# An MLP cut into pieces that stand between the attention tiles of two transformer layers

## The reference

```
# layer 0
h = ada_rms(x, cond, ln1_w, ln1_tw)
q, k, v = h @ Wq.T, h @ Wk.T, h @ Wv.T          # 8 query heads of 64, 1 key/value head
q, k = rope(q), rope(k)
x = x + softmax(q k / 8) v @ Wo.T               # within each entry of 64 tokens
h = ada_rms(x, cond, ln2_w, ln2_tw)
x = x + (silu(h @ Wg.T) * (h @ Wu.T)) @ Wd.T    # 512 -> 2048 -> 512
# layer 1
h = layernorm(x) * (1 + scale(cond)) + shift(cond)
q = h @ Wq1.T                                   # 16 query heads of 32
c_kv = h @ Wkd.T                                # latent of 128
k, v = c_kv @ Wku.T, c_kv @ Wvu.T               # 4 key/value heads
out = x + softmax(rope(q) rope(k) / sqrt(32)) v @ Wo1.T
```

## Time and profile before

| | |
|---|---|
| median of 3 timed runs | 1047.96 us (1046.9 to 1049.42) |
| span of the profiled execution | 1046.1 us |
| TensorE matmul busy | 934.1 us, 89% |
| VectorE busy | 575.7 us, 55% |
| ScalarE busy | 356.5 us, 34% |
| GpSimd busy | 219.1 us, 21% |
| mean granted TensorE clock | 0.960 |
| moved by DMA | 30.72 MB |

### The profile page before, as it was taken

One profiled execution on the slowest core, in us unless ns is written; L12 is line 12 of the kernel. 1 busy time (PEld: TensorE's weight loads), 2 busy tenths in 40 slices (PEclk: granted clock), 3 DMA queues, 4 the chain that ended last, 5 costly groups with the idle time before them and its releaser, 6 DMA issues.

```text
span 1046.1 us, 17609 instructions
## 1 busy us (share of the span) xinstructions
PE 934.1 (89%) x6400; PEld 790.3 (76%) x6400; DVE 575.7 (55%) x1019; ACT 356.5 (34%) x749; POOL 219.1 (21%) x174
## 2 busy tenths in 40 slices
PE   3889888988999999999999999999975788888876
PEld 3877777776888888888888888888865777777764
DVE  3056666663444444444444444444455688878884
ACT  4136555553221212112221122211124455555531
POOL 1324444541111101111211112111012122212210
PEclk9679999998999999999999999999997899999998
DMA  8400000000411001010110101100000000000000
GB/s 289 161 1 2 1 0 0 0 1 1 141 31 31 0 30 30 30 30 0 66 40 30 30 0 30 30 0 0 1 1 1 1 23 21 21 10 20 21 22 31
DMA packets 30741, 30.72 MB, mean 29 GB/s; under 512 B 3696, under 2 KB 20976, under 8 KB 30704
## 3 DMA queue, kind: packets, MB, share of 16 engines
q1 hardware_dynamic: 30704, 30.22, 8.9%
HBM read 26.02 MB, written 4.19 MB: 29 GB/s over the span
## 4 chain that ended last, share of the span: by engine, by line
PE 71%; issue 9%; DVE 8%; ACT 5%; POOL 4%; DMA 1%; ACTq 0%; SPq 0%; DVEq 0%; POOLq 0%
PE ps L397 21%; PE ps L399 21%; PE ps L398 21%; PE ps L405 3%; POOL yl L376 2%; DVE ex L803 1%; PE ps L474 1%; DVE xres L814 1%; DVE ex L794 1%; ACT yf L1118 1%; DVE smx L791 1%; DVE smx L798 1%; PE ps L631 1%; PE ps L565 1%; ACT ex L1028 1%
## 5 line engine op out<-in xcount | busy, mean ns | idle before, releaser
L397 PE MATMUL ps<-h2h,mwh 128*128 128x512 f32 x512 | 199.4, 389 | 0.0
L398 PE MATMUL ps<-h2h,mwl 128*128 128x512 f32 x512 | 199.2, 389 | 0.0
L399 PE MATMUL ps<-h2l,mwh 128*128 128x512 f32 x512 | 199.2, 389 | 0.0
L823 DVE TENSOR_TENSOR af<-ps,sg 128x512 f32<-128x512 f32 x64 | 44.3, 692 | 225.4 <-issue 212.4
L832 DVE TENSOR_TENSOR xres<-ps,xres 128x512 f32<-128x512 f32 x256 | 159.1, 682 | 2.1 <-PE ps L399 2.0
L344 POOL TENSOR_TENSOR mwl<-mst,mwh 128x1536 fp32r<-128x1536 f32 x16 | 56.1, 3509 | 373.1 <-ACT mwh L1062 373.1
L1068 ACT ACTIVATE sg<-ps 128x512 f32<-128x512 f32 x64 | 38.2, 598 | 216.8 <-PE ps L399 216.7
L398 PEld LDWEIGHTS ps<-h2h,mwl 128*128 128x128 f32 x512 | 96.1, 188 | 20.0
L399 PEld LDWEIGHTS ps<-h2l,mwh 128*128 128x128 f32 x512 | 96.1, 188 | 19.9
L397 PEld LDWEIGHTS ps<-h2h,mwh 128*128 128x128 f32 x512 | 96.1, 188 | 19.9
L1072 ACT CAST ah<-af 128x512 fp32r<-128x512 f32 x64 | 39.8, 621 | 188.1 <-DVE af L823 188.1
(11 more groups left out here) (161 smaller groups left out, 1737.8 us busy)
## 6 DMA issues: line engine op xcount, KB each, us to landing
mst<-WgT SPq DMA_DIRECT2D x16, 256.0 KB, 2.7
mst<-WuT SPq DMA_DIRECT2D x16, 256.0 KB, 3.1
mst<-WdT SPq DMA_DIRECT2D x16, 256.0 KB, 3.4
out<-fin SPq DMA_DIRECT2D x16, 256.0 KB, 2.0
xres<-x SPq DMA_DIRECT2D x1, 2560.0 KB, 20.9
adaw<-ln_twT SPq DMA_DIRECT2D x2, 1024.0 KB, 9.4
adaw<-adaT SPq DMA_DIRECT2D x1, 2048.0 KB, 14.6
wst<-WqT SPq DMA_DIRECT2D x1, 1024.0 KB, 9.1
```

Of the source, the lines that this page charges most:

```text
L397: pe.matmul(dst, lh, rh, start=start, stop=False)
L398: pe.matmul(dst, ll, rh, start=False, stop=False)
L399: return pe.matmul(dst, lh, rl, start=False, stop=stop)
L823: dve.tensor_tensor(af[:, :], bank(3 + r % 2), sg[:, :], ALU.mult).then_inc(m_af, 1)
```

## The change

The three stages become one. The MLP's outer loop now runs over the four blocks of 512 tokens and the inner one over the 16 groups, so the first block can be worked on when only the first four tiles have left layer 0's attention. Its work is written as a generator `mlp()` on each engine that stops (`yield`) after each piece: gate (12 matmuls), the first half of the step before's down (6), up (12), the other half (6). There are 256 pieces. `fill(pieces, count)` puts the next ones between the parts of the attention tiles, in numbers given by `FILL0` (three places in a step of layer 0) and `FILL1` (five places in a step of layer 1).

- The weights of a group are loaded, rounded and split once per block, 64 times instead of 16, gate and up as one array `gu` that is laid out on the host, down apart. `h2h` and `h2l` hold two blocks instead of four.
- `PREP0`, `LATE_PREP` and `PREP1` say in which step a tile's MLP input is made. The inputs of tiles 12 to 15 are made within layer 1's steps.
- Attention of both layers uses banks 0 to 3 (`XB`), the MLP 4 to 7: one for gate, one for up, two for down. Tiles 13 and 15 of layer 1 use banks 4 to 7 (`YB`).
- The small matmuls of the adaptive scales are spread over steps 0 to 3 (`adaptive_later`).
- Layer 1's latent is folded away: four matmuls of `Wkd` with the key and value weights (`keys_values_weights`) make weights of 256 columns, and `qkv1` has 24 matmuls of 384 columns. `latent_T`, `keys_values`, `key_rope` and the splits of the latent go. The repeated keys are summed by GpSimd (`rope_sum1`).
- Layer 1's output is summed into `xres` and stored from there.
- All hardware loops become straight code.

```diff
-TB_TOKENS = 512
...
+TB = 512
...
+FILL0 = {5: (4, 4, 4), **{s: (4, 4, 4) for s in range(6, 15)}, 15: (4, 5, 4)}
+FILL1 = {-1: (1, 4, 0, 4, 3), **{u: (3, 2, 2, 2, 2) for u in range(0, 9)}, 9: (3, 2, 2, 2, 3)}
+
+PREP0 = {2: 0, 3: 1, 4: 2, 6: 4, 7: 5, 8: 6, 9: 7, 11: 8, 12: 9, 13: 10, 14: 11}
+LATE_PREP = {4: 3}
+PREP1 = {0: 12, 1: 13, 2: 14, 3: 15}
...
+def fill(pieces, count):
+    for _ in range(count):
+        next(pieces, None)
...
+        XB = (0, 1, 2, 3)
+        BG, BU, BD = 4, 5, (6, 7)
+        YB = (4, 5, 6, 7)
...
+            def load_group(n):
+                g, i = n % NG, n % 2
+                wait(sp, m_gul, n - 1)
+                sp.dma_start(rgu[i][:, :], gu[g, :, :]).then_inc(ld_gu[i], 16)
+                wait(sp, m_wdl, n - 1)
+                sp.dma_start(rwd[i][:, :], WdT[g * P:(g + 1) * P, :]).then_inc(ld_wd[i], 16)
...
+            def down(n, i_from, i_to):
+                pe.wait_ge(m_al, n + 1)
+                pe.wait_ge(m_wdl, n + 1)
...
+                for i in range(i_from, i_to):
+                    wait(pe, m_x, n * TPB + i - 1)
+                    f = slice(P * i, P * (i + 1))
+                    three(bank(BD[i % 2]), ah[n % 2][:, f], al[n % 2][:, f], wdh[n % 2][:, :],
+                          wdl[n % 2][:, :], True, True).then_inc(m_down, 1)
+
+            def mlp():
+                for n in range(NN):
...
+                    pe.wait_ge(m_gul, n + 1)
+                    for w, to_bank, done in ((0, BG, m_gate), (1, BU, m_up)):
+                        if w == 0:
+                            wait(pe, m_sg, n)
+                        else:
+                            wait(pe, m_af, n)
+                        for k in range(KT):
+                            f = slice(P * (KT * w + k), P * (KT * w + k + 1))
+                            mm = three(bank(to_bank), guh[i][:, f], gul[i][:, f], h2h[b % 2][:, k, :],
+                                       h2l[b % 2][:, k, :], k == 0, k == KT - 1)
+                        mm.then_inc(done, 1)
+                        yield
+                        if n:
+                            down(n - 1, 2 * w, 2 * w + 2)
+                            yield
...
+            for s in range(-2, NT):
+                f1, f2, f3 = FILL0.get(s, (0, 0, 0))
+                if in_layer(s):
+                    scores(s)
+                if in_layer(s + 1):
+                    qkv(s + 1)
+                if s in PREP0:
+                    pe.wait_ge(a_ds, s + 1)
+                    x2_T(PREP0[s], XB[3])
+                fill(pieces, f1)
+                if in_layer(s):
+                    p_T(s)
+                if in_layer(s - 1):
+                    project(s - 1)
+                adaptive_later(s)
+                fill(pieces, f2)
+                if s == NT - 1:
+                    keys_values_weights()
+                if in_layer(s + 1):
+                    qk_T(s + 1)
+                if in_layer(s):
+                    context(s)
+                if in_layer(s + 2):
+                    x_T(s + 2)
...
+                fill(pieces, f3)
+            for u in range(-1, NT + 1):
+                f1, f2, f3, f4, f5 = FILL1.get(u, (0,) * 5)
+                if in_layer(u):
+                    scores1(u)
+                fill(pieces, f1)
+                if in_layer(u + 1):
+                    qkv1(u + 1)
+                if u == -1:
+                    project(NT - 1)
+                if in_layer(u - 1):
+                    project1(u - 1)
+                fill(pieces, f2)
+                if in_layer(u):
+                    p_T1(u)
+                fill(pieces, f3)
+                if in_layer(u + 1):
+                    qk_T1(u + 1)
+                if in_layer(u):
+                    context1(u)
+                if in_layer(u + 2):
+                    y_T(u + 2)
+                fill(pieces, f4)
...
+                fill(pieces, f5)
...
+            def mlp():
+                for n in range(NN):
+                    yield
+                    if n:
+                        add_down(n - 1, 0)
+                        add_down(n - 1, 1)
+                        yield
+                    dve.wait_ge(m_sg, n + 1)
+                    dve.wait_ge(m_up, n + 1)
+                    wait(dve, m_ah, n)
+                    wait(dve, m_al, n)
+                    dve.tensor_tensor(af[:, :], bank(BU), sg[:, :], ALU.mult).then_inc(m_af, 1)
+                    if n == 0:
+                        low_act(n)
+                    yield
+                    if n:
+                        add_down(n - 1, 2)
+                        low_act(n)
+                        add_down(n - 1, 3)
+                        yield
...
+                if in_layer(u + 2):
+                    stats1(u + 2)
+                if in_layer(u):
+                    softmax_sub1(u)
+                    softmax_norm1(u)
+                if in_layer(u + 2):
+                    mean_rstd(u + 2)
+                fill(pieces, f1)
+                if in_layer(u + 1):
+                    rope_mul1(u + 1)
```

More of the change, by code:

```diff
@@ L297, in _ @@
+            sp.wait_ge(w1f, 1)
+            sp.dma_start(w1st[:, :].rearrange("p (k n) -> p k n", k=KT), by_row(Wo1T)).then_inc(ld_w1, 16)
+            for u in range(0, NT + 1):
+                done += sum(FILL1.get(u, ()))
+                while n < min(done // 4 + 3, NN):
+                    load_group(n)
+                    n += 1
+                if u:
+                    store(u - 1)
+            assert n == NN
+            sp.wait_ge(b_st, 16 * NT)
         @block.gpsimd
@@ L385, in clear_bdv1 @@
+                wait(pool, b_qkT, t)
+                for c in range(2):
+                    key = lambda tile: tile[:, c, 8:10, :].unsqueeze(2).broadcast_to([P, 2, 4, HD1])
+                    pool.tensor_tensor(kr1[:, c, :, :, :], key(u1), key(u2), ALU.add)
+                query = lambda tile: tile[:, :, 0:8, :].rearrange("p c h d -> p c (h d)")
+                pool.tensor_tensor(qr1[:, :, :], query(u1), query(u2), ALU.add).then_inc(b_qks, 1)
             def clear_bdv1():
-                pool.wait_ge(m_x, NG * NT)
+                pool.wait_ge(a_rope, NT)
@@ new lines, in _ @@
+            for u in range(-1, NT):
+                f1, f2, f3, f4, f5 = FILL1.get(u, (0,) * 5)
+                ready, soon = PREP1.get(u), PREP1.get(u + 1)
+                if in_layer(u + 2):
+                    rstd1(u + 2)
+                fill(pieces, f1)
+                if in_layer(u + 1):
+                    rope_sum1(u + 1)
+                fill(pieces, f2 + f3)
+                if in_layer(u + 2):
+                    low_y(u + 2)
+                fill(pieces, f4)
+                if ready is not None:
+                    low_h2(ready)
+                if soon is not None:
+                    rstd2(soon)
+                if u == -1:
+                    low_w1_out()
+                fill(pieces, f5)
@@ L541, in _ @@
-            run_tiles(pe, NT, [(x_T, 2), (scores, 0), (qkv, 1), (x2_T, -2), (p_T, 0),
-                               (project, -1), (qk_T, 1), (context, 0)],
-                      {0: adaptive_rest, NT: lambda: gate_up(0, 0, 0, True),
-                       NT + 1: lambda: gate_up(0, 1, 0, True)})
-            pe.wait_ge(a_gf, NT)
-            down(0, 0, 0)
-            for r in range(2, NBLK):
-                gate_up(0, r, 0, True)
-                down(r - 1, (r - 1) % 2, 0)
-            with pe.Fori(0, NG // 2 - 1) as pair:
-                group(pair * 2 + 1, 1)
-                group(pair * 2 + 2, 0)
@@ L553, in _ @@
-            group(NG - 1, 1)
-            def y_T(t):
-                wait(pe, b_xn, t.n + 1)
-                if isinstance(t.n, int) and t.n == 0:
-                    pe.wait_ge(m_af, NG * NBLK - 1)
-                else:
-                    wait(pe, b_yf, t.n)
-                    wait(pe, b_ch, t.n - 3)
-                    wait(pe, b_cl, t.n - 3)
-                for k in range(KT):
-                    mm = pe.transpose(y_bank(t)[:, P * k:P * (k + 1)], yn[:, P * k:P * (k + 1)], idn[:, :])
-                mm.then_inc(b_xT, 1)
@@ new lines, in _ @@
+            for u in range(-1, NT):
+                f1, f2, f3, f4, f5 = FILL1.get(u, (0,) * 5)
+                ready, soon = PREP1.get(u), PREP1.get(u + 1)
+                if in_layer(u):
+                    softmax_exp1(u)
+                fill(pieces, f1)
+                if in_layer(u + 2):
+                    norm1(u + 2)
+                if in_layer(u + 1):
+                    values1(u + 1)
+                fill(pieces, f2)
+                if in_layer(u):
+                    probs_T1(u)
+                fill(pieces, f3)
+                if in_layer(u + 1):
+                    queries_keys1(u + 1)
+                if in_layer(u):
+                    high_ctx1(u)
+                if in_layer(u + 2):
+                    scale_shift_y(u + 2)
+                    high_y(u + 2)
+                fill(pieces, f4)
+                if ready is not None:
```

(8 more changed lines are left out.)

1301 lines of the change are left out of this document (689 added, 612 removed).

## The result

The changed kernel takes 1055.26 us (median of 4, 1051.89 to 1056.71), the kernel before 1047.43 beside it: a ratio of 1.0070, 95% interval 1.0052 to 1.0088. Run again later, unaltered, it took 1054.76 (ratio 1.0060, 1.0038 to 1.0082). It is 0.7% slower where I forecast 3% faster. The time lies within the range, at its upper end; the sign is wrong.

A forecast was written before the change was run, and what follows sets the result against it. TensorE has nothing to issue for about 155 us, nearly all outside the MLP. Start 132, filled work 751, stalls 26 and tail 105 sum to 1014, plus 1.9: 1016 us, 3% less, range 985 to 1056.

The forecast's parts named there:

- Filled work: TensorE's own time in the filled steps: 109 us in layer 0, 120 in layer 1, 522 for the MLP, 751.
- Stalls: TensorE's waits in the filled steps, mainly down matmuls for VectorE in layer 1 and in step 15: 26 us, bounds 0 and 88.
- Weights per block: Loading, rounding and splitting MLP weights 64 times instead of 16, on DMA, ScalarE and GpSimd: costed at 0.
- Table loads and straight code: 42 Exp/Silu table loads in ScalarE's idle time, 0, bound 54 us; unrolled loops, 0, left to the range.
- Start: Unfilled steps 0 to 4 of layer 0, 13.4 us each, plus small matmuls and half clock: filled steps start at 132 us.
- Tail: Unfilled tiles 10 to 15 of layer 1, steps of 15 to 19 us: 105 us, bounds 90 and 118.
- the first: Rival: TensorE never waits in the filled part and the clock recovers, 983 us; chance 0.20.
- the third: Rival: each of 42 ScalarE table loads delays a softmax or gate by 1.28 us, up to 1070 us; chance 0.05.
- The second: Rival: VectorE's order costs each of 21 filled steps, 4.2 us each giving 1078, 3.5 on average 1064; chance 0.17.
- The fourth: Rival: start at 145 and tail at 118 eat the gain, no change against the kernel before; chance 0.06.
- signs of being wrong: Tile 5's scores below 122 or above 142; waits for weights, DMA or Silu; over 3 us per filled step; tail over 118.
- Layer 1's step 10: Sign of being right: step 10, the first unfilled one in layer 1, begins at about 909 us.

The follow-up runs named there:

- kernel 11: Changed kernel with the edits of experiment 5, weight splits held as in experiment 10, step 15's query-weight split held too: 976.7 us, ratio to kernel before 0.9310.
- experiment 8: Changed kernel with GpSimd's low halves of MLP weights cut to 16 columns for the last 48 of 64 groups: 1041.5 us, ratio to kernel before 0.9935.
- experiment 10: Changed kernel with GpSimd's gate and up weight splits held until VectorE has formed `al` of two groups before: 1044.6 us, ratio to kernel before 0.9972.
- Experiment 1: Changed kernel with VectorE doing the first filling's MLP work before softmax reciprocal and scaling in layer 1: 1025.5 us, ratio to kernel before 0.9802.
- experiment 7: Changed kernel with Silu replaced by Identity, so the 42 table loads of the filled steps go: 1053.1 us, ratio to kernel before 1.0027.
- Experiment 6: Changed kernel with all 96 small matmuls ahead of tile 0's scores again: 1059.2 us, ratio to kernel before 1.0105.
- experiment 3: Changed kernel with own PSUM banks and an earlier input transpose in layer 0's steps 0 to 4: 1034.8 us, ratio to kernel before 0.9885.
- experiment 4: Changed kernel with tiles 11, 13, 15 on the other banks and earlier transposes for tiles 12 to 15: 1035.6 us, ratio to kernel before 0.9907.
- experiment 5: Changed kernel with the edits of Experiment 1, experiment 3, experiment 4, and GpSimd's statistics first in step 15: 979.8 us, ratio to kernel before 0.9351.

## Why the prediction was wrong

*The view of what bounds the kernel was right*, and so was the kind of gain: only the time outside the MLP could be won, and the middle won 38 us. The step that failed is the price of what stays outside the filling, and of what the filled steps do to each other. By the terms of the sum, with kernel 11 as the measure of pure work:

- **Filled work**, 751: kernel 11 takes 349.4 + 67.6 + 343.4 = 760.4 for the same part, with 3.7 us of waits for `al` in the whole run. 9 us too low: 3.6 in layer 0's ten steps (10.1 and 12 pieces of 2.04 give 34.6 for one, against 34.95), and most of the rest in layer 1's ten steps, for which the terms give 338 where 343.4 was measured. (0.227 scaled to 384 columns is 0.170, not 0.174, a slip of 0.1 us per tile; the trace has 0.174.)
- **Stalls**, 26: 800.5 - 760.4 = 40. The profile's waits for VectorE in this part make 32 of it, and the rest is mostly the clock. The places were right: the down matmuls of steps 0, 2, 4, 6, 8 for VectorE, and one wait in step 15 (5.4 us by the profile, 6 predicted). Steps 2 and 6 came out nearly as written (2.2 and 2.0 for 2.6). Steps 0, 4 and 8 waited 6.6 instead of 4.2. Without the meetings with GpSimd's splits they wait 3.4 (experiments 8 and 10), so my chain was 0.8 too long and the meetings, which it didn't have, add 3.2. The other part I left out altogether: after such a wait TensorE runs at half clock for a while. In step 0 the first three starts of 512-column matmuls from 577.75 on take 1.45 us, 0.48 each, where the pitch was 0.227. The granted clock by windows, around the wait from 571.1 to 577.75, reads:

```profile
566.00:570.00 4.00, 4.00 (x78) 3.39 (x79) 3.83 (x7) 2.83 (x4) 3.54 (x3) 1.00 0.00 0
...
577.70:579.00 1.30, 1.25 (x3) 1.05 (x4) 0.60 (x1) 0.00 (x0) 0.00 (x0) 0.50 0.91 260
579.00:581.00 2.00, 2.00 (x6) 1.61 (x6) 0.97 (x2) 0.00 (x0) 0.00 (x0) 0.50 0.48 197
581.00:583.00 2.00, 2.00 (x13) 2.00 (x12) 0.41 (x1) 0.00 (x0) 0.00 (x0) 0.99 0.00 0
```

  I counted half clock in the start and the tail and not here. Experiment 1 puts it at 9 us for layer 1, and experiment 10 shows that it doesn't shrink with these waits.
- **Weights per block**, 0: loads and roundings were hidden, as said, and no matmul waited for a weight of the MLP. GpSimd's splits were not free: 13.3 us by experiment 8. I looked only for a late result. The cost came through what the split does to VectorE while it runs. The Trainium skill has this rule: "SBUF — State Buffer", section "Who interferes with whom", says that a VectorE instruction with two inputs in SBUF and a GpSimd instruction that reads SBUF exclude each other, and that whichever started first makes the other wait for its full length. The trace agrees: 3.40 us instead of 1.22 behind a split, 3.76 instead of 0.69 behind the longer one, and no slowing for the sum with an operand in PSUM. The kernel before had few such meetings, since GpSimd had 16 splits of the MLP's weights instead of 128: there one subtraction of 64 is long (2.23 us) and no scaling.
- **Table loads and straight code**, 0: the loads lay in idle time (experiment 7), at 1.283 us each; the Trainium skill's 2.66 us for a switch ("ScalarE: Activation LUTs", section on what ACT_TABLE_LOAD costs) shows nowhere here. Its rule to do all calls of one set first stands in the page's section on table sets, not in the one that the prediction names; it would have been worth at most the 1.7 us of experiment 7. Straight code wasn't tried alone; layer 0's step at 34.95 against a computed 34.6 leaves at most 0.35 us for it there.
- **Start**, 132: came at 140.6. My 13.4 us for an unfilled step was too low. Experiment 6, with no small matmuls in these steps, needs 81.2 us for the five where I had 64, 17 more. The small matmuls and the half clock around them, for which I had 19.6 + 8, took the other way 17.1 (98.3 - 81.2, from one execution each), 10 less. The two errors partly hide each other, so it is luck that the start came as near as 8.6 us. The long wait list of the start (the scores for the scaled transpose of line 813, 7.6 us in 5 waits; the MLP's late preparation for ScalarE, 4.9; the projection for the scaled MLP input of line 819, 4.6) is the doing of the shared banks and of the order that goes with them: experiment 3, which changes both, gives 19.3 us back (12.2 against the quicker start).
- **Tail**, 105: 112.1, which experiment 4 turns into 92.9. The chain was rightly described and 7 us short: the steps took 20.5, 18.7, 16.8, 19.0, 17.3 and 19.8.

*Of the rivals*, the first (never waits) and the third (table loads) didn't happen. The second (VectorE decides in every step) happened in the five steps where I had put waits and, but for 1 us in step 9, in no other. The fourth, start and tail eat the gain, is the nearest: it had 145 and 118 at their bounds where 140.6 and 112.1 were measured, and 784 for the filled part where 800.5 came. I gave it 0.06; it takes both at their upper bounds. But start, tail, stalls and work were all built on the same assumption, that an order written for a full machine runs as tightly as the old one, and here the four errors had one sign and added up: 8.6 + 7.1 + 14.1 + 9.4 = 39.2 us.

*Of the signs of being wrong* none appeared, though the change loses: tile 5's scores at 140.6 lie below 142, the waits are 1.6 us per filled step and not 3, no matmul waited for a weight of the MLP or for Silu, and the tail is below 118. Each bound was set for one term alone. Start, tail and waits could err by 10, 13 and 37 us without touching theirs, and the whole gain was 32. Layer 1's step 10 was the plain sign, at 941.1 instead of 909.

## What to carry to other kernels

When work is moved between the parts of another loop, look first at the iterations that get none of it: they run with the order and the buffers of the filled ones, and here paid 45 us for 38 won. A filling of TensorE must not stand behind a softmax in VectorE's order when it needs VectorE itself, and a stall in mid-stream is to be priced with the half clock behind it. An engine with time to spare isn't free: see which operations of VectorE GpSimd's reads overlap, and whether those read two operands from SBUF.

## What the runs showed of the hardware

*The price of a small matmul follows the clock.* 54 took 11 us at half clock, 0.204 each; among full matmuls in the changed kernel's step 2, at a granted clock of 1.00, 24 take 2.6 us until the next instruction, 0.108 each:

```profile
95.37 2.76 PE L427 MATMUL ps<-condt,adaw 128*128 128x32 f32 x24
97.97 0.64 PE L470 MATMUL ps<-idn,qr 128*128 128x128 f32 x4
```

I had taken 19.6 us for the 96 wherever they stand.

*The same start, two clocks.* The changed kernel and experiment 1 have the same code on all engines until layer 1, and yet in the same 20 us of the start the granted clock and TensorE's count are:

```profile
80.00:100.00 20.00, 15.56 (x115) 14.24 (x113) 7.59 (x15) 7.02 (x17) 5.23 (x6) 0.83 0.01 2
```

```profile
80.00:100.00 20.00, 15.12 (x128) 13.85 (x129) 8.59 (x17) 8.71 (x19) 6.56 (x9) 1.00 0.00 1
```

The first is the changed kernel, with tile 5 at 140.6, the second experiment 1, with tile 5 at 133.5. Over the whole stretch from tile 0's scores to tile 5's, TensorE stands uncovered for 24.7 us in the one and 25.5 in the other, so the difference is the clock's alone. The timed runs of experiment 7 fall into two groups too: 1044.1 and 1046.1, and eight from 1051.2 to 1053.6. The changed kernel run again, unaltered, took 1050.1 and 1051.9 and then four times 1054.7 to 1057.7, not as clearly apart. The times lie within 3 us in experiments 3, 5 and 11, which wait less in the start, but also in experiments 6 and 8, which don't. What decides between the two patterns stays open.
